# Two batches of the second attention joined into one for 13 of its 16 steps

## The reference

```python
xn = rms_norm(x, gamma)
qkv = xn @ w_qkv                                   # 16 heads of 64
sim = jnp.einsum('bhid,bhjd->bhij', q * 64 ** -0.5, k)
attn = jax.nn.softmax(sim, axis=-1)
out = jnp.einsum('bhij,bhjd->bhid', attn, v)
return rearranged(out) @ w_out
```

## Time and profile before

| | |
|---|---|
| Median of 3 runs (1127.23 to 1127.7) | 1127.46 us |
| The profiled execution | 1127.43 us |
| Its span, first to last instruction | 1125.5 us |
| PE busy | 1103.9 us (98%) |
| POOL, DVE, ACT busy | 794.3, 846.5, 589.7 us |
| Steps 2 to 14 of the second attention | 541.47 us |

### The profile page before, as it was taken

The page is one execution under the profiler, slowest core; times in us unless marked ns, Lnnn a source line. Parts: engine busy times, 40 slices in busy tenths (PEclk is TensorE's granted clock), DMA queues, the critical chain, the costliest instruction groups (busy, mean ns, idle before and its releaser), DMA issues.

```text
span 1125.5 us, 21158 instructions
## 1 busy us (share of the span) xinstructions
PE 1103.9 (98%) x8392; PEld 705.8 (63%) x8392; DVE 846.5 (75%) x1250; ACT 589.7 (52%) x936; POOL 794.3 (71%) x522
## 2 busy tenths in 40 slices
PE   9999999999989999999999999999999999999998
PEld 7789888887755555455455454555555455457886
DVE  4676897666675878878888788887887888896554
ACT  4443333467657555555555465465555555554443
POOL 4777887754437888988888888988888898950000
PEclk9999999999989999999999999999999999999999
DMA  7322222220000002000000000000000000000000
GB/s 244 130 77 77 94 78 77 86 69 1 1 0 1 1 1 92 13 1 1 1 1 1 1 1 1 1 1 1 1 1 1 1 1 1 1 1 10 3 7 20
DMA packets 25601, 30.97 MB, mean 28 GB/s; under 512 B 2064, under 2 KB 21904, under 8 KB 24224
## 3 DMA queue, kind: packets, MB, share of 16 engines
q1 hardware_dynamic: 25184, 29.62, 7.8%
q10 hardware_dynamic: 320, 0.01, 0.0%
HBM read 20.19 MB, written 9.44 MB: 26 GB/s over the span
## 4 chain that ended last, share of the span: by engine, by line
PE 89%; DVE 8%; issue 2%; ACT 2%; POOL 0%; DVEq 0%; ACTq 0%; POOLq 0%
PE o_ps L1673 19%; PE mx_ps L1628 7%; PE st_ps L1657 5%; PE st_ps L1651 5%; PE st_ps L1654 5%; PE ha_banks L628 5%; PE bank L2069 3%; PE bank L2071 3%; PE bank L2070 3%; PE ha_banks L676 3%; PE mx_ps L1566 3%; PE pj_ps L1585 2%; PE ha_banks L687 2%; PE pj_ps L1577 2%; PE ha_banks L648 2%
## 5 line engine op out<-in xcount | busy, mean ns | idle before, releaser
L1983 POOL TENSOR_TENSOR acc<-acc,prob 128x1024 f32<-128x1024 f32 x192 | 468.4, 2440 | 63.2 <-ACT prob L1807 53.0
L1807 ACT ACTIVATE prob<-st_ps 128x1024 f32<-128x1024 f32 x256 | 248.5, 1022 | 209.3 <-PE st_ps L1657 209.3
L1673 PE MATMUL o_ps<-prob,v_cur 128*64 128x512 f32 x1024 | 245.6, 599 | 0.0
L1878 DVE TENSOR_REDUCE mx_part<-mx_ps 128x1 f32<-128x512 f32 x258 | 164.9, 667 | 72.4 <-PE mx_ps L1628 72.4
L1881 DVE TENSOR_REDUCE mx_part<-mx_ps 128x2 f32<-128x1024 f32 x79 | 94.9, 1201 | 45.1 <-PE mx_ps L1628 45.1
L1673 PEld LDWEIGHTS o_ps<-prob,v_cur 128*64 128x64 f32 x1024 | 68.0, 136 | 96.3 <-issue 77.5
L1897 DVE RECIPROCAL rden<-rden 128x128 f32<-128x128 f32 x128 | 120.6, 943 | 0.0
L1628 PEld LDWEIGHTS mx_ps<-k_hi,q_hi 64*128 64x128 f32 x416 | 47.0, 184 | 107.0 <-issue 95.4
L1628 PE MATMUL mx_ps<-k_hi,q_hi 64*128 64x512 f32 x416 | 112.7, 459 | 1.3 <-DVE mx_part L1881 1.1
L1657 PE MATMUL st_ps<-q_hi,d_lo 64*128 64x512 f32 x512 | 101.2, 392 | 0.0
L1983 POOL TENSOR_TENSOR acc<-prob 128x1024 f32<-128x1024 f32 x32 | 76.1, 2379 | 30.0 <-PE pj_ps L1562 19.0
(11 more groups left out here) (413 smaller groups left out, 2369.4 us busy)
## 6 DMA issues: line engine op xcount, KB each, us to landing
v_rows<-ha_v SPq DMA_DIRECT2D x8, 1024.0 KB, 3.9
ha_vt<-v_rows SPq DMA_DIRECT2D x16, 512.0 KB, 4.0
h_w<-in_h SPq DMA_DIRECT2D x2, 1024.0 KB, 7.4
w_raw<-in_w SPq DMA_DIRECT2D x8, 192.0 KB, 3.5
head_wkv<-in_wkv SPq DMA_DIRECT2D x2, 512.0 KB, 4.7
m_w<-in_m SPq DMA_DIRECT2D x3, 256.0 KB, 3.1
out<-fin SPq DMA_DIRECT2D x3, 256.0 KB, 2.3
sel_raw<-in_sel SPq DMA_DIRECT2D x1, 576.0 KB, 9.7
```

What stands on the lines that cost most here:

```text
L1673: mm = pe.matmul(o_ps[rows(h), :], v_cur[:, m % 2, j, rows(h)], prob[:, (16 * m + slot) % RING, h, :], start=(j == 0), stop=(j == KT - 1), ...
L1807: act.activation(prob[:, n % RING, :, :], st_ps[:, slot % 2, :, :], ACT.Exp, scale=SCALE).then_inc(s_exp, 1)
L1878: dve.reduce_max(mx_part[:, h, i, keys:keys + 1], maxima_banks(q, n)[h], AX_X).then_inc(s_mxr, 1)
L1983: pool.tensor_tensor(total, old, new, ALU.add).then_inc(s_acc, 1)
```

## The change

In steps 2 to 14 (`joined`) batches b and b + 1, b even, become one: `tensor_joined`, `scalar_joined` and `vector_joined`. PE now writes in one run the maxima and scores of both batches, then the outputs of four slots, and the units of the joined batch (`JOINED`) behind or between them. The first two q/k units of `BEFORE` (`QK[0]`, `QK[1]`) and the last (`QK[3]`) stand together in joined batch 0, `QK[2]` in joined batch 4. The four maxima of a joined batch use `mx_ps` both, `pj_ps` and `mx_ps` 0, `mx_ps` 1 and `pj_ps`, `mx_ps` both (`place_of` 0 to 3). ACT does four exponentials and then the copies of the units; DVE does the readings of all four maxima, then two reciprocals, then the units. POOL's order is the same. The other steps are untouched.

```diff
+    JOINED = {0: (QK[0], QK[3], QK[1], ("den", 1)), 2: (("tr", 1), ("out", 0), ("v", 0)),
+              4: (QK[2], ("den", 0)), 6: (("tr", 0), ("out", 1), ("v", 1))}
...
+        return 2 <= m < STEPS - 1
+
+    def joined_bank(q, u):
+
+        if not joined(q - AHEAD[u]):
+            return None
+        if u in (QK[1], QK[2]) or u[0] == "out":
+            return 0
+        return 1 if u in (QK[3], ("den", 0)) or u[0] == "tr" else None
...
+    def place_of(q, n):
+
+        m, b = batch_of(q, n)
+        return b % 2 * 2 + (n % 2 == 0) if joined(m) else None
+
     def apart(q, n):
 
-        return three(*batch_of(q, n))
+        return three(*batch_of(q, n)) or place_of(q, n) in (1, 2)
...
         if u[0] == "max":
-            pe.wait_ge(s_mxr, all_out[q, u[1]])
+
+            pe.wait_ge(s_mxr, (first_out if place_of(q, u[1]) == 1 else all_out)[q, u[1]])
...
+        if place_of(q, n) == 1:
+            return [pj_ps[:, :], mx_ps[:, 0, :]]
+        if place_of(q, n) == 2:
+            return [mx_ps[:, 1, :], pj_ps[:, :]]
...
+        elif place_of(q, n) in (1, 2):
+
+            m, b = batch_of(q, n)
+            pe.wait_ge(s_mxr, all_out[maximum(m, b & ~1, 0)])
+            bank_free(pe, turn_of[q, ("max", n)])
+        elif place_of(q, n) == 3:
+
+            pe.wait_ge(s_mxr, first_out[maximum(*batch_of(q, n), 0)])
...
+    def tensor_joined(pe, m, b):
+
+        for n in range(2):
+            tensor_maxima(pe, *maximum(m, b + n, 0))
+            tensor_scores(pe, m, 2 * (b + n))
+            if n:
+                tensor_maxima(pe, *maximum(m, b + n, 1))
+            tensor_scores(pe, m, 2 * (b + n) + 1)
+            if not n:
+                tensor_maxima(pe, *maximum(m, b + n, 1))
+        last = 16 * m + 2 * b - 2
+        for n in range(2):
+            tensor_outputs(pe, (last + n) // 16, (last + n) % 16)
+
+        between = {0: 3, 4: 2}.get(b, 0)
+        for unit in ends(m, b)[:between]:
+            tensor_unit(pe, *unit)
+        for n in range(2, 4):
+            tensor_outputs(pe, (last + n) // 16, (last + n) % 16)
+        for unit in ends(m, b)[between:]:
+            tensor_unit(pe, *unit)
...
+    def scalar_joined(act, m, b):
+        for slot in range(2 * b, 2 * b + 4):
+            scalar_exp(act, m, slot)
+        if b == 4:
+            scalar_keep(act, m, 0)
+        elif b == 0:
+            scalar_keep(act, m - 1, 1)
+        if b == 2:
+            scalar_differences(act, m + 1)
+        for unit in ends(m, b):
+            scalar_unit(act, *unit)
...
+    def vector_joined(dve, m, b):
+        for n in range(2):
+            vector_maxima(dve, *maximum(m, b + n, 0))
...
+            vector_maxima(dve, *maximum(m, b + n, 1))
+        vector_invert(dve, m, b)
+        vector_invert(dve, m, b + 1)
+        for q, u in ends(m, b):
...
+        if b % 4 == 0:
+            vector_normalize(dve, m - 1, b // 4)
```

More of the change, by code:

```diff
@@ L1437, in three @@
     def three(m, b):
-        return m >= 1 and b % (BATCHES // 2) != 0 and BATCHES * m + b < BATCHES * (STEPS - 1) + 3
+        return m >= 1 and not joined(m) and b % (BATCHES // 2) != 0 and BATCHES * m + b < BATCHES * (STEPS - 1) + 3
     def batch_of(q, n):
@@ L1547, in tensor_unit @@
             pe.wait_ge(s_row, 1)
+        elif joined_bank(q, u) is not None:
+            b = [at for at, units in JOINED.items() if u in units][0]
+            pe.wait_ge(s_mxr, all_out[maximum(q - AHEAD[u], b + 1, 1)])
         elif aside(q, u):
@@ L1576, in tensor_unit @@
             for h in range(2):
-                mm = pe.matmul(pj_ps[rows(h), :], c.ones[:, 0:HD], acc[:, half, h, :],
+                mm = pe.matmul(to[rows(h), :], c.ones[:, 0:HD], acc[:, half, h, :],
                                start=True, stop=True, skip_group_check=True)
@@ L1584, in tensor_unit @@
             for h in range(2):
-                mm = pe.matmul(pj_ps[rows(h), :], wo[:, p, rows(h)], o_n[:, half, :], start=True, stop=True,
+                mm = pe.matmul(to[rows(h), :], wo[:, p, rows(h)], o_n[:, half, :], start=True, stop=True,
                                skip_group_check=True)
@@ L1622, in tensor_maxima @@
             was = divmod(BATCHES * m + b - 1, BATCHES)
+            if n % 2 and joined(was[0]):
+                for unit in ends(was[0], was[1] & ~1):
+                    if joined_bank(*unit) is not None:
+                        unit_out(pe, *unit)
             if n % 2 and three(*was) and before(*was):
@@ L1735, in unit_bank @@
             return st_ps[:, 0, 0, :]
+        if joined_bank(q, u) is not None:
+            return mx_ps[:, joined_bank(q, u), :]
         return mx_ps[:, 1, :] if aside(q, u) else pj_ps[:, :]
@@ L1770, in scalar_unit @@
             act.wait_ge(s_pj, count_of[q, u])
-            act.activation(rden[:, half, :], pj_ps[:, :], ACT.Copy).then_inc(s_den, 1)
+            act.activation(rden[:, half, :], unit_bank(q, u), ACT.Copy).then_inc(s_den, 1)
     def scalar_differences(act, q):
@@ L1921, in vector_begin @@
         e.vector_norm(dve, LAST, "new")
+    def vector_joined(dve, m, b):
+        for n in range(2):
+            vector_maxima(dve, *maximum(m, b + n, 0))
+            if (n, b) == (0, 0) and not joined(m - 1):
+                vector_add_out(dve, *after(m - 1, BATCHES - 1))
+            vector_maxima(dve, *maximum(m, b + n, 1))
+        vector_invert(dve, m, b)
+        vector_invert(dve, m, b + 1)
+        for q, u in ends(m, b):
+            if u[0] == "qk":
+                vector_low(dve, q, u)
+            elif u[0] == "tr":
+                vector_spread_max(dve, q, u)
+            elif u[0] == "out":
+                vector_add_out(dve, q, u)
+        if b % 4 == 0:
+            vector_normalize(dve, m - 1, b // 4)
     def vector(dve, m, b):
+        if joined(m):
+            if b % 2 == 0:
+                vector_joined(dve, m, b)
+            return
         first, second = maximum(m, b, 0), maximum(m, b, 1)
@@ L1927, in vector @@
         was = (m, b - 1) if b else (m - 1, BATCHES - 1)
-        if after(*was) and AFTER[was[1]][0] == "out":
+        if after(*was) and AFTER[was[1]][0] == "out" and not joined(was[0]):
             vector_add_out(dve, *after(*was))
```

48 lines of the change are left out of this document (35 added, 13 removed).

## The result

| | before | changed |
|---|---|---|
| Median | 1127.35 us | 1198.14 us (1197.0 to 1199.26) |
| Ratio | 1 | 1.0627, 95% interval 1.0613 to 1.0642 |
| Profiled execution, its span | 1127.43, 1125.5 | 1197.39, 1195.5 |
| Steps 2 to 14 | 541.47 us | 611.98 us |

The kernel became 6.3% slower, 70 us in the profiled executions, and the 13 joined steps account for all of it: 611.98 - 541.47 = 70.5. Forecast were 1184 and 56.6 more.

A forecast was written before the change was run, and what follows sets the result against it. PE was taken to bound steps 2 to 14; 77.7 us of waits less 21.1 from fewer changes of kind gave 56.6 more, 1127.4 to 1184.0 us, range 1160 to 1200.

The forecast's parts named there:

- Part 1: PE's fewer changes of product kind cost 2.08 us a step instead of 3.70, a gain of 21.1 us.
- Outputs to q: PE's change from output products to q's in joined batches 0 and 4, taken as 0.21 us, bounds 0.13 and 0.56.
- Part 2: PE's waits in the longer runs for DVE's readings of the maxima's banks: 5.98 us a step, 77.7 in 13 steps.
- M1 to M2: Second to third maxima of a run, sharing pj_ps: 1.16 us where PE needs 0.23, costing 1.04 with the late next product.
- M2 to M3: Third to fourth maxima of a run, sharing bank 1 of mx_ps: 1.27 us where PE needs 1.03, costing 0.35.
- M1 behind M0: Second maxima start 1.82 us behind the first, costing 0.21 in joined batches 2 and 6, no wait in 0 and 4.
- a dearer change of kind: Upper bound of the range: PE's change from outputs to q costs the larger 0.56 us, adding 9 us.
- The cover of the exponentials: ACT's first of four exponentials is done 2.5 us into a run, before the third scores at 3.7; otherwise 0.1 thin.
- The faster one: Rival: only the fewer changes of kind count and the handover of pj_ps hides; 1106.3 us, chance 0.04.
- The shorter waits: Rival: in a run only second to third maxima wait, 0.93 us, as loads slip ahead; 1154.7 us, chance 0.08.
- More waits: Rival: the next run's first maxima wait behind out or q, or outputs to q costs 0.56; 1200 to 1209, chance 0.07.
- The clock: PE's clock might drop in the new steps; given little, as PE would stand still 0.93 us at most.

The follow-up runs named there:

- the first experiment: Against the changed kernel, the third maxima of a run wait once, for pj_ps, and the fourth wait for s_mxr ahead of older waits; 1193.4 us.
- the first two experiments: Each against the changed kernel: fewer separate waits before the third and fourth maxima, 1193.4 us; DVE reading 256 of 512 columns of the second maxima's pj_ps, 1187.2 us.

## Why the prediction was right, point by point

- **The bound and the count** held. PE bounds the stretch, and the count of products and changes closes the changed kernel too, to 0.1 us outside the runs.
- **Part 1** held. Outputs to q, which no row had shown, costs what I took for it:

```profile
751.34 1.94 PE L1736 MATMUL o_ps<-prob,v_cur 128*64 128x512 f32 x8
753.20 0.50 PE L1606 MATMUL pj_ps<-xr_hi,w_hi 128*128 128x512 f32 x1
753.54 0.39 PE L1607 MATMUL pj_ps<-xr_lo,w_hi 128*128 128x512 f32 x1
```

  751.34 to 753.20 is 1.86, that is 1.76 and 0.10, then 0.34 instead of 0.23: 0.21.
- **Part 2** named the right waits and the right order of their size, but was too small: 5.98 us a step against 7.0. The term that was mis-sized is the handover. M1 to M2 was put at 1.16 in all four runs and was 1.30, 1.38, 1.29 and 1.38; M2 to M3 at 1.27 and was 1.28, 1.38, 1.37 and 1.38. Two steps of the sum failed. For M2, and for M3 outside joined batch 0, I took 0.05 from the end of a reading to the next load from the earlier trace rows, where the wait is carried by the load; behind a wait instruction of its own it was 0.12 to 0.15, as the first experiment showed. And I took the end of M1 as 0.39 after its start, though my own M1 of joined batches 2 and 6 came out of a wait and then ends 0.50 after it, as M2 does: the two stalls weren't carried into each other. Together 1.0 us a step, or 13.6 of the 14 us that were missing.
- **M1 behind M0** in joined batch 2 was 1.95 instead of 1.82, 1.7 us in all, as it was late in steps 9 to 14. The cover by DVE's room, 12 us in a step, was counted as a sum. At this place `o_n` ran into the reading of M0. With it the terms are 15.3 us over mine, where 13.9 were missing. What stands against it is a double count: the 0.11 that I put behind M1 in joined batches 2 and 6 costs nothing, as M2 waits anyway, 2.9 us in all; and the stretches between the runs took 23.7 a step instead of 23.6, 1.4 us. 15.3 - 2.9 + 1.4 = 13.8.
- **Some luck in the range.** 1198 lies 2 us under its upper end. That end was made of 6 us for longer handovers and 9 for a dearer change of kind. The handovers took 13.6 more and the dearer change didn't come, so the range held by their sum and not by its terms.
- **The cover of the exponentials** held in the changed kernel and was indeed thin: with a slot between M1 and M2, s2 waits for the exponential of slot 0.
- **The rivals.** The faster one lost its case at M2's wait; what it says of the order alone is the count, of which no run shows more than 3 us. The shorter waits didn't come: the load of M2 starts with its product, at 761.64 and 761.67, and not ahead of the wait. "More waits" came near in time (1198 against 1200 to 1209), by a mechanism that it didn't name. The clock was granted in full over the 13 steps of the profiled execution, but the first experiment's profile shows that it can fall in these runs, for some 1.6 us each time, so it deserved more than the little that I gave it.
- **The marks.** PE busy 90.7% (about 90 forecast); the joined batches of step 9 12.7, 11.6, 11.4 and 11.3 us (12.6, 11.3, 11.3, 11.2; these add up to 46.4, where the sum had 46.0 a step).

## What to carry to other kernels

Longer runs of one kind save what a change of kind costs, here 0.13 to 0.21 us, but they take away the other work that covered the handover of a PSUM bank. Before joining, write down for each bank its writer, its reader and its next writer, and see that between the two writers stands at least one handover of PE's own work, here 1.2 to 1.4 us for 512 columns; moving one slot between two pairs of maxima gave back more than half of the loss. Let the wait that ends last be the one that the waiting instruction carries itself.

## What the runs showed of the hardware

A wait that was an instruction of its own made a handover 0.09 us longer than one that the load carries, 1.30 against 1.21 us, though it ends at the same reading.

DVE's `o_n`, the only large operation of DVE in the joined steps with both inputs in SBUF, takes 0.68 to 0.69 us or, if it starts well before the end of one of POOL's additions, until 0.55 us behind that end: in the changed kernel 16 of its 32 took 0.68 or 0.69, and the other 16, 1.3 to 2.0 us long, all ended 0.55 to 0.56 behind POOL's. In the changed kernel (DVE and POOL around the end of a joined batch 0), POOL's second addition ends at 753.71 + 4.84 = 758.55 and `o_n` at 757.35 + 1.75 = 759.10:

```profile
757.35 1.75 DVE L2014 TENSOR_TENSOR o_n<-o_sum,rden 128x512 f32<-128x512 f32 x1
...
753.71 4.84 POOL L2116 TENSOR_TENSOR acc<-acc,prob 128x1024 f32<-128x1024 f32 x2
```

In the kernel with no shared bank it is 2.71 us, and ends 0.54 behind POOL's addition (654.78 + 4.81 = 659.59, 657.42 + 2.71 = 660.13):

```profile
654.78 4.81 POOL L2120 TENSOR_TENSOR acc<-acc,prob 128x1024 f32<-128x1024 f32 x2
...
657.42 2.71 DVE L2018 TENSOR_TENSOR o_n<-o_sum,rden 128x512 f32<-128x512 f32 x1
```

In the kernel with the short reading of M1 it is 2.28 us at the same place, ends 0.55 behind POOL (745.95 + 4.84 = 750.79, 749.06 + 2.28 = 751.34), and so the reading of M0 (PE started M0 at 749.90) comes 1.36 us behind it, at 751.26, instead of 0.54:

```profile
745.95 4.84 POOL L2119 TENSOR_TENSOR acc<-acc,prob 128x1024 f32<-128x1024 f32 x2
...
749.06 2.28 DVE L2017 TENSOR_TENSOR o_n<-o_sum,rden 128x512 f32<-128x512 f32 x1
751.26 1.21 DVE L1994 TENSOR_REDUCE mx_part<-mx_ps 128x2 f32<-128x1024 f32 x1
```

The Trainium skill (SBUF — State Buffer, SBUF: two separate sides) has the rule for it: a DVE operation with two SBUF inputs and a GpSimd one that reads SBUF exclude each other for the whole instruction. The traces agree for the case in which POOL's is first. I had not weighed it, and it is why DVE was late for M0 where its summed room said that it had time. In the changed kernel and the first two experiments M1 of joined batch 2 is late in steps 9 to 14 alone, and ahead of it `o_n` meets an addition in these six steps alone: M1 is 2.05 to 2.17 behind M0 in the changed kernel, 2.32 to 2.43 with the wait on the product and 2.62 to 2.71 with the short reading. So a part of these two gains was lost again there. No run took POOL's additions away.
